# Attention beside a mixture of experts: output chunks spread over a batch, and the row of maxima issued from ScalarE

## The reference

```python
xn = _layernorm(x)
q, k, v = (xn @ W + b for W, b in ((Wq, bq), (Wk, bk), (Wv, bv)))     # 16 heads of 16
probs = softmax(einsum('bqhd,bkhd->bhqk', q, k) * 16 ** -0.5)
attn = einsum('bhqk,bkhd->bqhd', probs, v).reshape(B, T, 256) @ Wo + bo
x1 = _layer_norm(xn + attn, ln1_g, ln1_b)                            # then router and experts
```

## Time and profile before

| | |
|---|---|
| median of 3 runs | 2176.37 us (2168.57 to 2180.98) |
| profiled execution | 2177.51 us, its span 2175.7 us |
| mean granted clock of TensorE | 0.913 |
| TensorE matmul busy | 1812.3 us, 83% |
| VectorE busy | 1287.6 us, 59% |
| GpSimd busy | 986.1 us, 45% |
| ScalarE busy | 839.2 us, 39% |
| the plain attention | from the start to about 758 us of the span |

### The profile page before, as it was taken

The page is one execution under the profiler, slowest core; times in us unless marked ns, Lnnn a source line. Parts: engine busy times, 40 slices in busy tenths (PEclk is TensorE's granted clock), DMA queues, the critical chain, the costliest instruction groups (busy, mean ns, idle before and its releaser), DMA issues.

```text
span 2175.7 us, 33971 instructions
## 1 busy us (share of the span) xinstructions
PE 1812.3 (83%) x11505; PEld 1085.2 (50%) x11506; DVE 1287.6 (59%) x2862; ACT 839.2 (39%) x1144; POOL 986.1 (45%) x624
## 2 busy tenths in 40 slices
PE   3877878778778406999669999999998998989998
PEld 1333424324334206999645554656556465554654
DVE  4665666566656343777676565665556665556561
ACT  1444455354445213454315334252442514325152
POOL 3113332332432553454435737376372854728554
PEclk8888989799889757999869999999999999989999
DMA  6335152262242153656420010100101001010000
GB/s 104 47 61 70 30 120 49 33 138 39 42 57 73 54 218 124 218 216 221 134 50 2 2 40 1 40 2 10 31 2 40 1 11 31 2 40 1 10 21 10
DMA packets 72277, 130.31 MB, mean 60 GB/s; under 512 B 11158, under 2 KB 50230, under 8 KB 66236
## 3 DMA queue, kind: packets, MB, share of 16 engines
q1 hardware_dynamic: 69052, 119.89, 21.9%
q0 software_dynamic: 3072, 8.39, 1.2%
HBM read 76.09 MB, written 26.74 MB: 47 GB/s over the span
## 4 chain that ended last, share of the span: by engine, by line
PE 37%; issue 7%; DVE 3%; POOL 2%; ACT 1%; DMA 0%; POOLq 0%; DVEq 0%; ACTq 0%; SPq 0%
PE a_psS L703 11%; PE a_psO L717 9%; PE a_psO L740 6%; PE a_psM L677 5%; PE a_psS L665 4%; PE a_psS L649 2%; PE a_psS L730 1%; POOL a_k_tok L350 1%; ACT a_probs L468 1%; DVE a_junk L534 1%; POOL a_oT L373 1%; POOL a_q_tok L350 1%; DVE a_alibi L611 0%; DVE a_rden L548 0%; DVE a_turned L542 0%
## 5 line engine op out<-in xcount | busy, mean ns | idle before, releaser
L385 POOL TENSOR_TENSOR a_probs<-a_probs 128x1024 f32<-128x1024 f32 x144 | 340.7, 2392 | 342.9 <-PE a_psO L717 342.9
L534 DVE CUSTOM_DVE_ANT_0 a_junk<-a_psM,a_alibi 128x512 bf16<-128x512 f32 x512 | 333.7, 689 | 241.3 <-PE a_psM L677 240.3
L1272 DVE TENSOR_REDUCE f_n_tok<-f_psR 128x1 f32<-128x512 f32 x512 | 320.7, 680 | 194.2 <-PE f_psR L1408 193.8
L468 ACT ACTIVATE a_probs<-a_psS 128x1024 f32<-128x1024 f32 x256 | 249.7, 1024 | 307.9 <-PE a_psS L703 307.7
L1216 ACT ACTIVATE f_probs<-f_psS 128x1024 f32<-128x1024 f32 x256 | 248.1, 1024 | 232.2 <-PE f_psS L1427 230.2
L717 PE MATMUL a_psO<-a_probs,a_v 128*32 128x512 f32 x2048 | 244.0, 597 | 0.0
L1408 PE MATMUL f_psR<-f_kP,f_qP 48*128 48x512 f32 x512 | 182.7, 522 | 58.3 <-DVE f_n_tok L1272 31.4
L1408 PEld LDWEIGHTS f_psR<-f_kP,f_qP 48*128 48x128 f32 x512 | 76.3, 202 | 204.2 <-DVE f_n_tok L1272 119.2
L1427 PE MATMUL f_psS<-f_qP,f_kP 64*128 64x512 f32 x512 | 101.5, 447 | 90.6 <-DMA f_qP<-f_n_row 89.7
L677 PE MATMUL a_psM<-a_kH,a_qH 64*128 64x512 f32 x512 | 128.9, 496 | 34.4 <-DVE a_n_tok L534 27.7
L1440 PE MATMUL f_psO<-f_probs,f_v 128*32 128x512 f32 x1024 | 152.7, 671 | 0.7 <-ACT f_probs L1216 0.6
(11 more groups left out here) (190 smaller groups left out, 3580.1 us busy)
## 6 DMA issues: line engine op xcount, KB each, us to landing
w_w_high<-w_parts SPq DMA_DIRECT2D x19, 1024.0 KB, 5.4
w_w_low<-w_parts SPq DMA_DIRECT2D x19, 1024.0 KB, 7.6
f_kP<-f_high SPq DMA_DIRECT2D x64, 128.0 KB, 4.4
f_qP<-f_high SPq DMA_DIRECT2D x64, 128.0 KB, 6.3
e_xs<-sorted_x SPq DMA_DIRECT2D x19, 256.0 KB, 2.7
sorted_z<-e_z SPq DMA_DIRECT2D x19, 256.0 KB, 2.2
sorted_x<-f_zeros SPq DMA_DIRECT2D x7, 640.0 KB, 9.2
f_xn<-in_L_attn_x SPq DMA_DIRECT2D x8, 512.0 KB, 3.9
```

What stands on the lines that cost most here:

```text
L385: nc.gpsimd.tensor_tensor(slots, slots, probs[:, first - GRP:first - GRP + 2, :], ALU.add).then_inc(added.sem, 1)
L468: nc.scalar.activation(probs[:, slots, :], psS[:, 2 * p:2 * p + 2, :], ACT.Exp).then_inc(exp_done.sem, 1)
L534: nc.vector.tensor_tensor_reduce(out=junk[:, a, :], in0=psM[:, a, :], in1=alibi[:, h, :], scale=1.0, scalar=-3.0e38, op0=ALU.add, op1=ALU.max,
L1272: nc.vector.tensor_reduce(n_tok[:, c, column:column + 1], psR[:, ring_bank("max", u), :], AX.X, ALU.max, negate=True).then_inc(max_done.se ...
```

## The change

The four output chunks leave quad 0 and are made in (2,0), (2,1), (2,3) and (3,0); so that they can be, `oT` gets a second buffer, and the second norm's statistics are taken in (3,1) instead of (2,3). The row of maxima is sent by ScalarE, right behind its own copy, and SyncE has nothing to do with it any more. The expert weights are loaded, split and stored in halves, one half in each batch, which makes room in SBUF. SyncE moves both groups of sides first in a batch. GpSimd makes the low parts ahead of the normalizations and adds the bias to the rows after them, and its two large memsets at the start wait for the normalized rows. The diff, with few lines around each place:

```diff
     HALVES = (slice(0, FB), slice(FB, P))
-    EXTRAS = {(0, 1): [("v", 1)], (0, 2): [("out", 0), ("out", 1)], (0, 3): [("out", 2), ("out", 3)],
-              (1, 0): [("proj", 0)], (1, 1): [("proj", 1)], (1, 2): [("maxima", 2), ("proj", 2)],
-              (1, 3): [("proj", 3)], (2, 2): [("maxima", 3)], (3, 2): [("maxima", 0)], (3, 3): [("v", 0)]}
-    EXTRAS[0, 2] = [("maxima", 1)] + EXTRAS[0, 2]
+    EXTRAS = {(0, 1): [("v", 1)], (0, 2): [("maxima", 1)], (1, 0): [("proj", 0)], (1, 1): [("proj", 1)],
+              (1, 2): [("maxima", 2), ("proj", 2)], (1, 3): [("proj", 3)], (2, 0): [("out", 0)], (2, 1): [("out", 1)],
+              (2, 2): [("maxima", 3)], (2, 3): [("out", 2)], (3, 0): [("out", 3)], (3, 2): [("maxima", 0)],
+              (3, 3): [("v", 0)]}
     TURNED = {(0, 3): [("rows", 0, 0), ("rows", 1, 2)]}
...
         rsum = sb("rsum", [P, S])
-        oT = sb("oT", [P, QUADS, S])
+        oT = sb("oT", [P, 2, QUADS, S])
         r1 = sb("r1", [P, TT, D])
-        w1_raw = sb("w1_raw", [P, KC, FF])
-        w1_high, w1_low = sb("w1_high", [P, KC, FF], F32R), sb("w1_low", [P, KC, FF], F32R)
+        w1_raw = sb("w1_raw", [P, FF])
+        w1_high, w1_low = sb("w1_high", [P, FF], F32R), sb("w1_low", [P, FF], F32R)
 
...
 
-            def move_maxima(b, quad):
-
-                sp.wait_ge(n_row_done.sem, n_row_done.at(b, quad))
-                first_place = place_of(b, QP * quad)
-                for a in range(2):
-                    row = FB * a + NEG
-                    sp.dma_start(qP[row:row + 1, first_place:first_place + QP, :].bitcast(F32),
-                                 n_row[QP * a:QP * (a + 1), quad % 2, :].bitcast(F32)).then_inc(n_moved.sem, 16)
-
-            def load_w1(e):
-                sp.dma_start(w1_raw[:, :, :], w["W1"][e].rearrange("(c p) n -> p c n", p=P)).then_inc(w1_in, 16)
-
-            def store_w1(e):
-                sp.wait_ge(w1_rest, e + 1)
+            def load_w1(n):
+                sp.dma_start(w1_raw[:, :], w["W1"][n // KC].rearrange("(c p) n -> c p n", p=P)[n % KC]).then_inc(w1_in, 16)
+
+            def store_w1(n):
+                sp.wait_ge(w1_rest, n + 1)
                 for part, tile in enumerate((w1_high, w1_low)):
-                    sp.dma_start(w1_parts[e, part], tile[:, :, :].rearrange("p c n -> p (c n)").bitcast(F32))\
-                        .then_inc(w1_stored, 16)
+                    sp.dma_start(w1_parts[n // KC, part].rearrange("p (c n) -> c p n", c=KC)[n % KC],
+                                 tile[:, :].bitcast(F32)).then_inc(w1_stored, 16)
 
...
             move_sides(0, 1)
-            move_maxima(0, 0)
             for tile, source in preloads:
...
                 more = b + 1 < B
-                move_maxima(b, 1)
+                if more:
+                    move_sides(b + 1, 0)
+                    move_sides(b + 1, 1)
+                if b:
+                    store_w1(b - 1)
+                load_w1(b)
+                clear_rows(b)
                 if b + 2 < B:
                     load_rows(b + 1)
-                if more:
-                    move_sides(b + 1, 0)
-                move_maxima(b, 2)
-                if more:
-                    move_sides(b + 1, 1)
-                move_maxima(b, 3)
-                if b % 2 == 0:
-                    if b:
-                        store_w1(b // 2 - 1)
-                    load_w1(b // 2)
-                clear_rows(b)
-                if more:
-                    move_maxima(b + 1, 0)
-
-            store_w1(NE - 1)
+
+            store_w1(B - 1)
             sp.wait_ge(cleared, 16 * B)
-            sp.wait_ge(w1_stored, 2 * NE * 16)
+            sp.wait_ge(w1_stored, 2 * KC * NE * 16)
 
...
             norm0.raise_variance(pool, 0)
+            pool.wait_ge(xn_done.sem, xn_done.at(0, TT - 1))
             nc.gpsimd.memset(kP[:, :, :].bitcast(F32), 1.0).then_inc(zeroed, 1)
...
                 pool.wait_ge(rsum_done.sem, rsum_done.at(b, quad))
-                nc.gpsimd.tensor_tensor(oT[:, quad, :], oT[:, quad, :], rsum[:, :], ALU.mult)\
+                nc.gpsimd.tensor_tensor(oT[:, b % 2, quad, :], oT[:, b % 2, quad, :], rsum[:, :], ALU.mult)\
                     .then_inc(norm_done.sem, 1)
...
             def split_w1(e):
+
                 pool.wait_ge(w1_in, 16 * (e + 1))
...
                     pool.wait_ge(w1_stored, 2 * 16 * e)
-                nc.gpsimd.tensor_copy(w1_high[:, :, :], w1_raw[:, :, :]).then_inc(w1_split, 1)
+                nc.gpsimd.tensor_copy(w1_high[:, :], w1_raw[:, :]).then_inc(w1_split, 1)
                 pool.wait_ge(w1_split, e + 1)
-                nc.gpsimd.tensor_tensor(w1_low[:, :, :], w1_raw[:, :, :], w1_high[:, :, :],
+                nc.gpsimd.tensor_tensor(w1_low[:, :], w1_raw[:, :], w1_high[:, :],
                                         ALU.subtract).then_inc(w1_rest, 1)
...
                     normalize(b - 1, QUADS - 1)
+                if more:
+                    low_part(b + 1, 0)
+                    low_part(b + 1, 1)
+                normalize(b, 0)
+                if more:
+                    low_part(b + 1, 2)
+                    low_part(b + 1, 3)
+                normalize(b, 1)
                 add_bias_to_rows(b, not before)
...
                     keep_rows(b + 1)
-                    low_part(b + 1, 0)
-                normalize(b, 0)
-                if more:
-                    low_part(b + 1, 1)
-                normalize(b, 1)
-                if more:
-                    low_part(b + 1, 2)
-                    low_part(b + 1, 3)
                 if before:
...
                     finish_rows(b - 1)
-                if b % 2:
-                    split_w1(b // 2)
+                split_w1(b)
 
...
                                psR[0:4, ring_bank("maxima", n), :]).then_inc(n_row_done.sem, 1)
+                act.wait_ge(n_row_done.sem, n_row_done.at(b, n))
+                place = place_of(b, QP * n)
+                for a in range(2):
+                    row = FB * a + NEG
+                    act.dma_start(qP[row:row + 1, place:place + QP, :].bitcast(F32),
+                                  n_row[QP * a:QP * (a + 1), n % 2, :].bitcast(F32)).then_inc(n_moved.sem, 16)
 
...
                 act.wait_ge(pv_done.sem, pv_done.at(b, TT * quad + TT - 1))
-                nc.scalar.copy(oT[:, quad, :], psO[:, :]).then_inc(o_taken.sem, 1)
+                nc.scalar.copy(oT[:, b % 2, quad, :], psO[:, :]).then_inc(o_taken.sem, 1)
 
...
                     if j == 0:
-                        if quad == 1 and before:
-                            act.wait_ge(out_ps.sem, out_ps.at(b - 1, TT - 1))
+                        if quad == 1 and b > 1:
+                            act.wait_ge(out_ps.sem, out_ps.at(b - 2, TT - 1))
                         if quad:
...
                 dve.wait_ge(o_taken.sem, o_taken.at(b, quad))
-                nc.vector.transpose(turned[:, :], oT[:, quad, :]).then_inc(turned_done.sem, 1)
+                nc.vector.transpose(turned[:, :], oT[:, b % 2, quad, :]).then_inc(turned_done.sem, 1)
                 dve.wait_ge(turned_done.sem, turned_done.at(b, quad))
...
                         norm0.apply(dve, b + 1, xn, xn, xn_done)
-                    if (quad, j) == (2, 3) and before:
+                    if (quad, j) == (3, 1) and before:
                         dve.wait_ge(r1_done.sem, r1_done.at(b - 1, TT - 1))
...
                 for quad in range(QUADS):
-                    last = nc.tensor.matmul(bank[:, 0:D], oT[:, quad, t * P:(t + 1) * P], wo[:, quad, :],
+                    last = nc.tensor.matmul(bank[:, 0:D], oT[:, b % 2, quad, t * P:(t + 1) * P], wo[:, quad, :],
                                             start=(quad == 0), stop=(quad == QUADS - 1))
```

## The result

The changed kernel takes 2118.85 us at the median of four runs (2113.64 to 2122.28), the kernel before 2178.68 beside it; the ratio is 0.9723 [0.967, 0.9775]. The forecast was 2088 with a range of 2055 to 2125: the direction held and the range too, but 2088 is 31 us too low. Its profiled execution took 2116.67 us (span 2114.5, granted clock 0.918), 60.8 less than the one of before, where 88.8 were forecast.

A forecast was written before the change was run, and what follows sets the result against it. TensorE, the busiest engine, with nearly 20 us of waits a batch, was taken as the bound. Start -7.1, batches 1 to 6 -77.7, batch 0 -10.6, last batch 0, tail +6.6 sum to -88.8: 2088 us, range 2055 to 2125.

The forecast's parts named there:

- The wait for the row: Plain attention, TensorE's wait for the row of maxima before scores: -12.6 us, plus 1.0 left, in seven batches.
- ScalarE's issues: ScalarE issuing the row's two transfers holds up its own next work: +1.0 us a batch, bounds 0 and 4.8.
- The chunks: Output chunks leave (0,2) and (0,3), -9.05 us a batch, and cost +5.2 in (2,0), (2,1), (2,3), (3,0).
- Rival (b): The chunks cost in quads 2 and 3 what they cost in quad 0: 2111 us; chance 0.12.
- The statistics in (3,1): Norm1's statistics, moved from (2,3), make (3,1) and (3,2) 1 to 2 us longer: +1.5 a batch, bounds 0 and 2.
- Start: Before the batches, memsets wait for normalized rows; the first side goes at 21.7 us instead of 28.76: -7.1.
- batch 0: First batch of the plain attention, which has no chunks: -12.6 + 2.0 = -10.6 us.
- tail: End of the plain attention: GpSimd's scaling starts later, so the last normalization comes later: +6.6 us, bounds +3 and +10.
- (c): Quad 3's row stays late behind sides and W1: 2.8 to 5 us instead of 1.0, 2101 to 2116; chance 0.12.
- (d): TensorE stays at its high clock: batches of 69 to 72 us instead of 74.8, 2054 to 2071; chance 0.12.
- (e): GpSimd's queue makes the raised variance late; VectorE, then TensorE, stand in (0,2): 2187 us at 20 late; chance 0.03.
- (f): Nothing gained, the waits merely change their name: about 2176 us; chance 0.01.

The follow-up runs named there:

- rows_only: The kernel before, with the row of maxima sent by ScalarE and nothing else changed; 2117.27 us, ratio 0.974.
- stats_moved: The kernel of rows_only with only the second norm's statistics moved from (2,3) to (3,1); 2147.46 us, ratio 0.987.
- stats_spread: The changed kernel with norm1's four statistics spread over (2,2), (2,3) and (3,0), none in (3,1); 2096.61 us, ratio 0.9635.
- all_gpsimd: The changed kernel with both norms' statistics spread, GpSimd's order changed in the last batch, and both norms' epsilon added by GpSimd; 2072.72 us, ratio 0.9507.
- spread_gpsimd: The kernel of stats_spread with norm1's addition of epsilon done by GpSimd instead of VectorE; 2106.01 us, ratio 0.9658.

## Why the prediction was right, and where its size was off

**The wait for the row** (-12.6 + 1.0 a batch): right. 89.7 us became 10.0. **ScalarE's issues** (+1.0): 1.16 to 1.30 a pair, as forecast, but they cost next to nothing. In rows_only and before, (0,2) and (0,3) of batch 0 take 8.02 and 7.95 together, and (1,2) 5.20 and 5.18 on the mean. That quad 0 still came out as forecast is chance: the chunks brought 8.7 instead of 9.05, the issues cost nothing, and (0,1) took 0.8 more. In the second profile (0,1) took 2.6 more, and quad 0 came out 6.1 shorter, not 8.05.

What stood behind the 1.0 for the wait was put less well: the packets of a row alone on the engines have passed 1.0 us after the end of issue (2.2 after its start), where the bound taken was 2.9, and those of one beside SyncE's backlog pass later. Two sections of the Trainium skill's "DMA: Bandwidth & Descriptors" were weighed there. In rows_only, batch 3, the row of quad 3 was issued from 351.09 to 352.27, and its eight packets passed between 354 and 356, while q1 kept the engines full until 358 (the windows of 354 to 355 and of 355 to 356):

```profile
q1 hardware_dynamic: 74, 0.12, 104.9%
q10 hardware_dynamic: 4, 0.00, 3.6%
...
q1 hardware_dynamic: 73, 0.12, 100.3%
q10 hardware_dynamic: 4, 0.00, 3.8%
```

So a queue of its own does get its turn among the other's packets, as the Trainium skill says in that page's section "Queues, rings and completion order", but the last of them passed up to 4.9 us after the start of issue instead of 2.2, and (3,0), which began at 357.69, waited 4.1 for it; that is nothing like nought. In the change itself (the rows above) that turn came only when the backlog ran out: from 338 to 339 q10 has no packet beside 361 of q1. What was gained there, 10.7 to 4.1 us of wait, is mostly the 5.9 us at the issuer. By the section "Issuing engines are not separate DMA queues" of the same page of the Trainium skill only such time on the sequencer can be gained; the trace agrees, with 5.9 at the issuer gone and 5.4 from the end of issue to use left of 5.6.

**The chunks** (-9.05 and +5.2): right as a pair. (2,0), (2,1), (2,3) less its wait, and (3,0) take 4.53, 4.62, 4.8 and 4.15, and (0,2) and (0,3) 3.43 and 4.62; (0,3) keeps 0.9 more than batch 0 of before. Rival (b), chunks at the price of quad 0, is out.

**The statistics in (3,1)** (+1.5): the step that failed. "(3,1) and (3,2) get longer by 1 to 2": they and (3,3) got 4.8 longer. The 3.3 a batch that this is more than forecast make 20 us in batches 1 to 6, where 18.6 are missing; the other steps came out 0.2 a batch better. I counted VectorE's 2 us of work once, as if TensorE's work behind it kept its price. But TensorE stood still behind it for 1.94 us, and then did (3,2) and (3,3) at a granted clock of 0.66 and 0.60. TensorE's busy time shows it: it stayed at 69 us a batch. From (0,2) to (3,0) it fell by 3.7, with a clock of 1.00 where (0,3) had 0.83; in (3,1) to (3,3) it rose by 2.8, and in (0,0) and (0,1) by 0.8.

The second profile of the change has the same sum in other places: 3.4 more in (3,1) to (3,3) (2.0 idle, 1.4 work) and 2.6 more in (0,0) and (0,1), where VectorE's addition of epsilon was held up. So the statistics cost 3.4 to 4.8 by two executions, and in the second 2.0 a batch are missing in quad 0, by (0,1), which the forecast left as it was.

Two runs test the burst. In stats_moved the same steps get 2.2 longer for a move of the statistics alone. That this is less than 3.4 to 4.8 fits a burst that costs more behind a (3,0) filled by a chunk, which no run isolates. In stats_spread (3,2) and (3,3), without the burst, fall by 2.7 to 4.2; but (3,1) rises by 2.8, so the sum of the three steps is still 3.4 above before. all_gpsimd takes away GpSimd's hold on VectorE as well: (3,1) to (3,3) take 1.6 more than before the change, about the forecast 1.5.

**Start, batch 0, tail**: -6.5, -10.9, +5.0 for -7.1, -10.6, +6.6. The chain through GpSimd's queue was right to 0.1 us where scaling starts.

**The rest**: of 28.0 us between 2088.7 and 2116.67, 17.3 are in the plain attention, 10.3 in phases that nothing touched, 0.4 outside the span. The 10.3 stay open; in the second profile they are 5.9.

**The rivals**: (c) happened, at 0.6 to 1.0 us in six batches and 2.4 in batch 0, instead of 2.8 to 5. (d) is false for this kernel, and all_gpsimd comes near it: batches of 72.9, where (d) has 69 to 72, and a clock of 0.98. (e) didn't happen, but what spoke for it, GpSimd holding up a VectorE instruction, made steps of TensorE 2 to 4 us longer where it hit for 1.5 us or more, and in one case 6.8. (f) is out.

## What to carry to other kernels

When an engine waits for a transfer, look first at what its issuer does before it: a transfer of 4 KB stood 5.9 us behind 128 KB ones in SyncE's order, and a change of issuer alone brought as much as a rewrite of the batch. Before work of a second engine is moved to where "there is room", count what it holds up: 2 us of VectorE in one piece cost TensorE 2.2 to 4.8 by three profiles, about half of it idle time and half slower products behind it. In four pieces it still cost 3.4, as its last small instruction was now held up by GpSimd; with that gone too, 1.6 were left. And before a gain is read from one profile, take a second one: here single steps of one program differed by 1.8 us a batch. And when several parts of a change are tried together, time each alone: here two of them removed the same wait.

## What the runs showed of the hardware that was not expected

- A VectorE `tensor_scalar` on 128 x 4 values takes 0.17 us, or up to 2.06 when one of GpSimd's 2.4 us instructions has begun before it, and 3.85 behind one of 4.50. Which of the two happens can differ between executions of one program (2.6 us or 11.3 us in total over 15), and where it was removed in one place (spread_gpsimd) it stood in another, with nothing won.
- At equal work, TensorE's busy time in six batches was 413.4, 401.3 or 390.8 us (granted clock 0.93, 0.95, 0.98), in the change, stats_spread and all_gpsimd, which differ in how VectorE's and GpSimd's small instructions lie beside it; 6 us of such a difference also lie between two executions of the change (413.4 and 407.5).
- The eight packets of a 4 KB pair, on a queue of their own, had passed 2.2 us after the start of issue on idle engines, and about 5 us after it beside a full queue.
